# A router's ranks over tiles added up by TensorE in place of VectorE's running sum

## What is computed

```python
xf = input.reshape(N, Dq)
probs = jax.nn.softmax(xf @ router_w + router_b, axis=-1)
eid = jnp.argmax(probs, axis=-1)
onehot = jax.nn.one_hot(eid, E, dtype=xf.dtype)
rank = (jnp.cumsum(onehot, axis=0)[jnp.arange(N), eid] - 1.0).astype(jnp.int32)
valid = rank < C
pos = jnp.where(valid, rank, 0)
vmask = valid.astype(xf.dtype)[:, None]
buf = jnp.zeros((E, C, Dq), xf.dtype).at[eid, pos].add(xf * vmask)
h = jax.nn.relu(jnp.einsum('ecd,edh->ech', buf, w1) + b1[:, None, :])
y = jnp.einsum('ech,ehd->ecd', h, w2) + b2[:, None, :]
y_tok = y[eid, pos] * vmask
yov = jax.nn.relu(xf @ ow1 + ob1) @ ow2 + ob2
out = y_tok + yov * (1.0 - vmask)
```

## Time and profile before

| | us |
|---|---|
| three runs shown | 1013.89, 1017.33, 1018.5 |
| median of them | 1017.33 |
| the profiled execution, its own time | 1013.49 |
| its span in the profile | 1011.7 |

### The profile page before, as it was taken

How to read it: one execution, slowest core, us unless ns; L and a number is a source line. 1 busy time by engine, 2 the same in 40 slices (tenths; PEclk the granted TensorE clock), 3 DMA queues, 4 the chain that set the end, 5 groups by cost and what they waited for, 6 DMA issues and landing times. The chain is left out here.

```text
span 1011.7 us, 17450 instructions
## 1 busy us (share of the span) xinstructions
PE 902.6 (89%) x5825; PEld 642.4 (63%) x5832; DVE 676.6 (67%) x1619; ACT 421.3 (42%) x1133; POOL 376.5 (37%) x279
## 2 busy tenths in 40 slices
PE   2899989999889985868899889999999839999997
PEld 2687744444478864743487547777777517778786
DVE  5899967987689988876377687878768631222221
ACT  2466640000155656753355345556664403122222
POOL 1676402433467722516455313333333410110111
PEclk9999999999999997988899999999999969999999
DMA  6100079999700008102366382311111148534200
GB/s 208 59 1 0 1 205 251 312 306 285 247 1 1 0 1 222 52 16 95 113 188 202 117 262 72 113 51 51 51 51 36 44 143 299 203 98 152 93 12 20
DMA packets 87260, 117.18 MB, mean 116 GB/s; under 512 B 12464, under 2 KB 75949, under 8 KB 86781
## 3 DMA queue, kind: packets, MB, share of 16 engines
q1 hardware_dynamic: 77455, 88.15, 29.4%
q10 hardware_dynamic: 4408, 15.46, 4.6%
q0 software_dynamic: 5328, 12.70, 3.5%
HBM read 68.08 MB, written 50.16 MB: 117 GB/s over the span
## 5 line engine op out<-in xcount | busy, mean ns | idle before, releaser
L1016 PE MATMUL psum<-m_W,lnT 128*128 128x512 f32 x256 | 114.2, 598 | 0.6 <-DVE acc L928 0.6
L410 POOL TENSOR_TENSOR prob<-prob,a_rden 128x1232 f32<-128x1232 f32 x30 | 67.5, 2250 | 58.1 <-DVE a_rden L506 58.1
L1016 PEld LDWEIGHTS psum<-m_W,lnT 128*128 128x128 f32 x256 | 47.2, 190 | 59.0 <-issue 55.8
L2907 ACT ACTIVATE prob<-psum,x_b 128x320 f32<-128x320 f32 x64 | 33.8, 527 | 120.8 <-PE psum L2964 120.8
L2575 PE MATMUL psum<-g_VW,pT 128*128 128x256 f32 (+1 forms) x320 | 72.5, 382 | 1.6 <-ACT pT L2465 1.5
L1001 POOL TENSOR_TENSOR m_masked<-m_rel,m_mrow 128x1232 f32<-128x1232 f32 x16 | 42.2, 2647 | 84.5 <-DMA masked_bias<-m_masked 62.2
L2765 POOL DMA_INDIRECT out_x<-x_yt,x_X x20 | 19.8, 992 | 137.3 <-DVE x_yt L2846 137.3
L2575 PEld LDWEIGHTS psum<-g_VW,pT 128*128 128x128 f32 (+1 forms) x320 | 59.5, 190 | 11.2 <-issue 3.7
L2234 POOL TENSOR_TENSOR g_qr<-g_t 128x1024 f32<-128x1024 f32 x15 | 35.5, 2364 | 74.1 <-DVE g_t L2307 74.1
L2527 PE MATMUL psum<-g_Wq,lnT 128*128 128x512 f32 x128 | 59.1, 605 | 1.0 <-ACT lnT L2439 1.0
L2241 POOL TENSOR_TENSOR prob<-prob,g_rden 128x1232 f32<-128x1232 f32 x15 | 33.7, 2248 | 68.3 <-DVE g_rden L2342 68.3
(11 more groups left out here) (472 smaller groups left out, 2240.7 us busy)
## 6 DMA issues: line engine op xcount, KB each, us to landing
routed_rows<-hole SPq DMA_DIRECT2D x8, 2210.0 KB, 36.8
masked_bias<-m_masked ACTq DMA_DIRECT2D x16, 616.0 KB, 8.2
g_bias<-masked_bias SPq DMA_DIRECT2D x16, 616.0 KB, 3.9
m_xb<-routed_rows SPq DMA_DIRECT2D x39, 130.0 KB, 2.0
m_rel<-in_rel_bias ACTq DMA_DIRECT2D x8, 616.0 KB, 10.9
expert_rows<-hole SPq DMA_DIRECT2D x1, 4680.0 KB, 36.7
g_early_w<-in_L_ffn_w SPq DMA_DIRECT2D x8, 512.0 KB, 4.7
g_early_w<-in_L_ffn_w SPq DMA_DIRECT2D x4, 1024.0 KB, 5.7
```

The lines of the kernel that those rows point to most:

```text
L410: nc.gpsimd.tensor_tensor(heads(c.prob[b]), heads(c.prob[b]), rden[b][:, :].unsqueeze(2).to_broadcast([P, H, SK]), ALU.mult).then_inc(norm ...
L1016: last = nt.matmul(c.ps[p][:, :], c.lnT[b][:, k * P:(k + 1) * P], W[:, k, p * 512:(p + 1) * 512], start=(k == 0), stop=(k == KC - 1))
```

## The change

`first_expert` writes the one-hot rows straight into `r.ohb` as bf16, and its cast is gone. `first_slot` is gone, with the padded buffers and their two memsets. TensorE adds up in one PSUM bank what VectorE's running sum did: for a tile it adds, to the triangular product of the tile itself, the all-ones product of every tile ahead of it. A product with a `shift` covers several tiles at once: columns of the tiles first to last get the counts of the tiles `shift` earlier. `pe_earlier_ranks` issues those that reach into earlier groups (before the group's one-hot rows are ready), `pe_ranks` the triangular one and those inside the group. In the last group one more block of columns, `wide`, gets the total counts.

Products per group: group 0 has 1 + 7 = 8 in place of 2. Group 1 has 11 in `pe_earlier_ranks` (shifts 4 to 8, 1 to 3, 9 to 11) and 1 + 3 = 4 in `pe_ranks`. Group 2 has 16 (shifts 5 to 12, 1 to 4, 13 to 16) and 1 + 4 = 5. `slots` has eight operations: two read PSUM, three are fused scalar-tensor-tensor operations.

```diff
 def first_expert(c, dve, r, u, logits, chain, read, nth=1):
-    lg, tmp, hot = c.lg[:, eights], c.lgt[:, eights], c.gates[:, eights]
+    lg, tmp, hot = c.lg[:, eights], c.lgt[:, eights], r.ohb[:, eights]
...
-    chain(nv.tensor_tensor(tiles(hot), tiles(tmp), wide(first), ALU.is_equal))
-    return nv.tensor_copy(r.ohb[:, eights], hot)
-
-
-def first_slot(c, r, u, chain):
-
-    nv = c.nc.vector
-    n, ones8, _ = group_of(u)
-    pre, first = r.pre, c.first[:, ones8]
-    if u > 0:
-        last_tile = slice((PAD + ROUTED[u - 1][1] - 1) * 8, (PAD + ROUTED[u - 1][1]) * 8)
-        for v in range(2):
-            chain(nv.tensor_copy(pre[v][:, (PAD - 1) * 8:PAD * 8], pre[1][:, last_tile]))
-    chain(nv.tensor_scalar(r.slotf[:, 0:n], first, -float(CAP), float(E3 * CAP), ALU.mult, ALU.add))
+    return nv.tensor_tensor(tiles(hot), tiles(tmp), wide(first), ALU.is_equal)
 
 def slots(c, dve, r, u, ranks, chain, read, nth=1):
...
-    nv.tensor_copy(before, ranks[:, 0:n * 8])
-    nv.tensor_copy(pre[0][:, data], ranks[:, n * 8:2 * n * 8]).then_inc(read, 1)
+    nv.tensor_scalar(over8, ranks[:, 0:n * 8], -float(CAP), 0.0, ALU.add, ALU.max)
+    nv.tensor_tensor(rank8, ranks[:, 0:n * 8], r.ohb[:, eights], ALU.mult).then_inc(read, 1)
     dve.wait_ge(read, nth)
-    chain(nv.tensor_tensor(pre[1][:, data], pre[0][:, data], pre[0][:, back(1)], ALU.add))
-    chain(nv.tensor_tensor(pre[0][:, data], pre[1][:, data], pre[1][:, back(2)], ALU.add))
-    chain(nv.tensor_tensor(pre[1][:, data], pre[0][:, data], pre[0][:, back(4)], ALU.add))
-    chain(nv.tensor_tensor(rank8, before, pre[1][:, back(1)], ALU.add))
-    chain(nv.tensor_scalar(over8, rank8, -float(CAP), 0.0, ALU.add, ALU.max))
-    chain(nv.tensor_tensor(rank8, rank8, hot, ALU.mult))
-    chain(nv.reduce_sum(orank, tiles(over8), AX))
+    nv.reduce_sum(over, tiles(over8), AX)
     chain(nv.reduce_sum(rank, tiles(rank8), AX))
-    chain(nv.tensor_scalar(orank, orank, float(E3 * CAP), None, ALU.add))
-    chain(nv.tensor_scalar(valid, rank, float(CAP), None, ALU.is_lt))
-    chain(nv.tensor_tensor(slotf, slotf, rank, ALU.add))
-    chain(nv.tensor_tensor(slotf, slotf, orank, ALU.subtract))
-    chain(nv.tensor_tensor(slotf, slotf, valid, ALU.mult))
-    return nv.tensor_tensor(r.slot[:, ones8], slotf, orank, ALU.add)
+    chain(nv.scalar_tensor_tensor(out=slotf, in0=c.first[:, ones8], scalar=-float(CAP), in1=rank, op0=ALU.mult, op1=ALU.add))
+    chain(nv.tensor_tensor(slotf, slotf, over, ALU.subtract))
+    chain(nv.scalar_tensor_tensor(out=slotf, in0=rank, scalar=float(CAP), in1=slotf, op0=ALU.is_lt, op1=ALU.mult))
+    return nv.scalar_tensor_tensor(out=r.slot[:, ones8], in0=slotf, scalar=float(E3 * CAP), in1=over, op0=ALU.add, op1=ALU.add)
 
+def rank_tiles(u):
+
+    lo, n = ROUTED[u]
+    return lo, n, n + (lo + n == NT)
+
+def pe_count(c, r, u, bank, shift, first, last, start=False):
+
+    lo = ROUTED[u][0]
+    return c.nc.tensor.matmul(bank[:, (first - lo) * 8:(last - lo) * 8], r.onesb, r.ohb[:, (first - shift) * 8:(last - shift) * 8],
+                              start=start, stop=True, skip_group_check=True)
+
+def pe_earlier_ranks(c, r, u, bank):
+
+    lo, n, wide = rank_tiles(u)
+    shifts = [*range(wide, lo + 1), *range(1, wide), *range(lo + 1, lo + wide)]
+    for shift in shifts:
+        pe_count(c, r, u, bank, shift, max(lo, shift), min(lo + wide, lo + shift), start=shift == shifts[0])
+
 def pe_ranks(c, r, u, bank):
 
-    n, _, cols = group_of(u)
-    c.nc.tensor.matmul(bank[:, 0:n * 8], r.upper, r.ohb[:, cols], start=True, stop=True)
-    return c.nc.tensor.matmul(bank[:, n * 8:2 * n * 8], r.onesb, r.ohb[:, cols], start=True, stop=True)
+    lo, n, wide = rank_tiles(u)
+    c.nc.tensor.matmul(bank[:, 0:n * 8], r.upper, r.ohb[:, lo * 8:(lo + n) * 8], start=u == 0, stop=True, skip_group_check=True)
+    for shift in range(1, wide):
+        last = pe_count(c, r, u, bank, shift, lo + shift, lo + wide)
+    return last
 
...
+                pe.wait_ge(s["s_used"], NT)
+                pe_earlier_ranks(c, r, 1, c.ps[0])
                 pe.wait_ge(s["r_oh_ok"], 2)
-                pe.wait_ge(s["s_used"], NT)
                 pe_ranks(c, r, 1, c.ps[0]).then_inc(s["r_pre_ps"], 1)
...
             first_expert(c, dve, rt, 2, bank_back[:, 0:2 * P], chain, s["lg_read"]).then_inc(s["oh_ok"], 1)
-            first_slot(c, rt, 2, chain)
...
-            chain(nv.tensor_scalar(cnt[:, :], rt.pre[1][0:1, (PAD + NT - LAST - 1) * 8:(PAD + NT - LAST) * 8], -float(CAP), 0.0, ALU.add, ALU.max))
+            chain(nv.tensor_scalar(cnt[:, :], bank_rank[0:1, (NT - LAST) * 8:(NT - LAST + 1) * 8], -float(CAP), 0.0, ALU.add, ALU.max))
...
             pe_logits_back(c, rt, 2, bank_back).then_inc(s["logits_ps"], 1)
+            pe_earlier_ranks(c, rt, 2, bank_rank)
             pe.wait_ge(s["oh_ok"], 1)
             pe_ranks(c, rt, 2, bank_rank).then_inc(s["pre_ps"], 1)
```

More of the change, by code:

```diff
@@ L1118, in __init__ @@
         self.ohb = c.lg2[:, 0:NT * 4].bitcast(BF16)
-        n = (PAD + HALF) * 8
-        self.pre = [c.acc[0][:, u * n:(u + 1) * n] for u in range(2)]
         m = HALF * 8
-        self.before = c.acc[0][:, 2 * n:2 * n + m]
         self.rank8, self.over8 = c.acc[1][:, 0:m], c.acc[1][:, m:2 * m]
-        self.rank, self.valid, self.orank, self.slotf = (c.acc[1][:, 2 * m + u * HALF:2 * m + (u + 1) * HALF] for u in range(4))
+        self.rank, self.over, self.slotf = (c.acc[1][:, 2 * m + u * HALF:2 * m + (u + 1) * HALF] for u in range(3))
         self.slot = c.acc[1][:, 2 * m + 4 * HALF:2 * m + 4 * HALF + NT].bitcast(U32)
@@ L1165, in slots @@
     n, ones8, eights = group_of(u)
[L1166 to L1170, removed]
-    nv.tensor_copy(before, ranks[:, 0:n * 8])
-    nv.tensor_copy(pre[0][:, data], ranks[:, n * 8:2 * n * 8]).then_inc(read, 1)
-    dve.wait_ge(read, nth)
-    chain(nv.tensor_tensor(pre[1][:, data], pre[0][:, data], pre[0][:, back(1)], ALU.add))
-    chain(nv.tensor_tensor(pre[0][:, data], pre[1][:, data], pre[1][:, back(2)], ALU.add))
-    chain(nv.tensor_tensor(pre[1][:, data], pre[0][:, data], pre[0][:, back(4)], ALU.add))
-    chain(nv.tensor_tensor(rank8, before, pre[1][:, back(1)], ALU.add))
-    chain(nv.tensor_scalar(over8, rank8, -float(CAP), 0.0, ALU.add, ALU.max))
-    chain(nv.tensor_tensor(rank8, rank8, hot, ALU.mult))
-    chain(nv.reduce_sum(orank, tiles(over8), AX))
-    chain(nv.reduce_sum(rank, tiles(rank8), AX))
-    chain(nv.tensor_scalar(orank, orank, float(E3 * CAP), None, ALU.add))
-    chain(nv.tensor_scalar(valid, rank, float(CAP), None, ALU.is_lt))
-    chain(nv.tensor_tensor(slotf, slotf, rank, ALU.add))
-    chain(nv.tensor_tensor(slotf, slotf, orank, ALU.subtract))
-    chain(nv.tensor_tensor(slotf, slotf, valid, ALU.mult))
-    return nv.tensor_tensor(r.slot[:, ones8], slotf, orank, ALU.add)
+    rank8, over8 = (t[:, 0:n * 8] for t in (r.rank8, r.over8))
+    rank, over, slotf = (t[:, 0:n] for t in (r.rank, r.over, r.slotf))
+    nv.tensor_scalar(over8, ranks[:, 0:n * 8], -float(CAP), 0.0, ALU.add, ALU.max)
+    nv.tensor_tensor(rank8, ranks[:, 0:n * 8], r.ohb[:, eights], ALU.mult).then_inc(read, 1)
+    dve.wait_ge(read, nth)
+    nv.reduce_sum(over, tiles(over8), AX)
+    chain(nv.reduce_sum(rank, tiles(rank8), AX))
+    chain(nv.scalar_tensor_tensor(out=slotf, in0=c.first[:, ones8], scalar=-float(CAP), in1=rank, op0=ALU.mult, op1=ALU.add))
+    chain(nv.tensor_tensor(slotf, slotf, over, ALU.subtract))
+    chain(nv.scalar_tensor_tensor(out=slotf, in0=rank, scalar=float(CAP), in1=slotf, op0=ALU.is_lt, op1=ALU.mult))
+    return nv.scalar_tensor_tensor(out=r.slot[:, ones8], in0=slotf, scalar=float(E3 * CAP), in1=over, op0=ALU.add, op1=ALU.add)
 def pe_logits(c, r, u, bank):
@@ L2363, in route @@
                 row_statistics(c, 0)
-                for u in range(2):
-                    nv.memset(r.pre[u][:, 0:PAD * 8], 0.0)
                 dve.wait_ge(s["r_in"], 16 * 3)
@@ L2379, in places @@
                 first_expert(c, dve, r, 0, c.ps[1][:, 0:2 * P], chain, s["r_lg_read"]).then_inc(s["r_oh_ok"], 1)
-                first_slot(c, r, 0, chain)
             if t == RANKS_AT:
@@ L2384, in places @@
             if t == HALF + 7:
-                first_slot(c, r, 1, chain)
                 dve.wait_ge(s["r_pre_ps"], 2)
```

## The result

Over 20 executions each, the median went from 1016.31 us to 1012.49 us. The ratio of the changed kernel to the one before is 0.9969, with a 95% interval from 0.9954 to 0.9984. On 1016.3 us that is 3.2 us less, between 1.6 and 4.7; the two medians differ by 3.8. One execution of the changed kernel, 1370.38 us at a mean granted clock of 0.652, is left out of the ratio. The forecast was 2.7 us less and 1014.6 us, with a range from 1010.5 to 1018: a small gain, and one under 0.5%. Both came true.

A forecast was written before the change was run, and what follows sets the result against it. The last router's serial VectorE chain ahead of the experts' matmuls was taken to bound the kernel, with TensorE limiting attention. Router 2.15 plus attention 0.52 made 2.7 us, so 1017.33 became 1014.6 us, range 1010.5 to 1018.

The forecast's parts named there:

- a longer wait for the landing: Last router: prediction wrong if the wait for the scatters' landing grows by what VectorE's chain lost.
- Part 1: Last router up to the ranks: removing the cast and `first_slot` starts `slots` 0.32 us earlier.
- Part 2: Last group's `slots`: 1.46 us in place of 3.29, a gain of 1.83 us.
- Part 3: First group inside attention: VectorE 2.2 us earlier, but TensorE's warming products let only 1.04 us through.
- Part 4: Second group inside attention: 13 more TensorE products on the path cost 0.52 us at 0.04 each.
- The clock: First expert's matmuls: moving their start could give back up to 1.7 us of half-clock loss or cost as much again.
- M: Rival: small TensorE products cost 0.07 us each; gain 2.0 us, 1015.3 us; chance 0.17.
- B: Rival: small TensorE products cost 0.11 us each; net gain 0.7 us, 1016.6 us; chance 0.14.
- D: Rival: load and product do not overlap, 0.29 us per small product; loss 6.3 us, 1023.6 us; chance 0.04.
- C: Rival: the clock over the first expert gives its stall back; gain 4.4 us, 1012.9 us; chance 0.14.
- its opposite: Rival: the clock over the first expert loses 1.7 us more, 1016.3 us; chance 0.07.
- E: Rival: last router gains nothing as said because GpSimd was not waiting for VectorE's chain; chance 0.02.

The follow-up runs named there:

- warm2: The changed kernel with 2 warming products in place of 10 ahead of the last attention tile's scores; ratio 0.9953 to the kernel before.
- the first pair: First traces of the kernel before and the changed kernel; the first expert's 32 matmuls took 10.32 and 11.75 us.
- the second: Both kernels traced again without edit; the first expert's 32 matmuls took 11.24 us before and 8.85 us changed.

## Why the prediction was right, and where it was off

**What bounds.** Right. The last router is a series in which VectorE's operations arrive one to one. The scatter came 0.27 us behind the chain before and after. Nothing took the place of what was removed: the first expert's matmuls came 13.91 us behind that scatter before and 13.37 after, so the sign against the forecast, a longer wait for the landing, did not show.

**Part 1, start of the chain.** Forecast 0.32 us, measured 2.42 - 2.06 = 0.36 (turned-back logits to `slots`, 811.77 to 814.19 and 811.15 to 813.21). The step is right. The price of 0.04 us per small product was too high: the last of the five started 0.10 us behind the first (812.89, then four over 812.93 to 813.17), not 0.16. The sixteen earlier products cost nothing, as said.

**Part 2, `slots`.** Forecast 1.46 us, measured 1.39. The gain was 1.90, not 1.83. The fused operations take 0.16 us, no more than the two-tensor ones of that width, and reading PSUM cost nothing.

**Part 3, first group.** The mechanism held: VectorE's chain was shorter, the rotation now starts at 774.30 when TensorE's queries end (770.58 + 3.68), and the warming products cap the gain, which warm2 showed. The rotation starts 2.85 us earlier (16.74 and 13.89 behind the start of A), where I had 2.2; behind the warming products that changed nothing. The stall I foresaw is there too: L1157 took 0.88 us, until GpSimd's multiply ended, as L1174 took 1.32 in the earlier trace rows. The Trainium skill ("GPSIMD Engine Reference", section "1. Specifications") says that VectorE contends with GpSimd for SBUF where it has two SBUF inputs, and the trace agrees: the sums just ahead, with one input, were not held up. The size was off: the scores start 1.49 us earlier, not 1.04. Two terms were missing. The first is 0.27 us ahead of the queries. I had booked that idle time as cover for six products and called the removed cast and `first_slot` of the first group "hidden by TensorE". They were not: their 0.42 us on VectorE bring ScalarE's copy L2439 forward by as much (from 10.02 to 9.60 us behind the start of A), and it was this copy that TensorE waited for. The products took back the other 0.15. The second is 0.18 us: the idle time shown ahead of the scores was 1.04, but more was to be had. Scores without a wait start at 785.61, which is 0.16 ahead of the last warming product's modelled end, 785.77; with the wait they started 1.05 behind it (784.62 and 785.67).

**Part 4, second group.** On the path, as forecast, but its cost was mis-sized. With 0.52 us I had 13 times 0.04. Before:

```profile
795.41 0.18 PE L1219 MATMUL psum<-lg,choice 128*128 128x32 bf16 x1
...
797.61 4.48 PE L2575 MATMUL psum<-g_VW,pT 128*128 128x256 f32 x20
```

After:

```profile
795.25 0.42 PE L1198 MATMUL psum<-lg,choice 128*128 128x32 bf16 x11
...
797.68 4.49 PE L2567 MATMUL psum<-g_VW,pT 128*128 128x256 f32 x20
```

Counted from the scores of tile 15, the last tile's products with the values start 797.61 - 785.67 = 11.94 us later before and 797.68 - 785.61 = 12.07 after: 0.13 us. The thirteen products themselves cost 0.28: from the first rank product to the last tile's transposes it was 795.93 - 795.41 = 0.52 us and is 796.05 - 795.25 = 0.80. The other 0.15 came back around them: 0.10 between the scores and the ranks (the scores behind the wait took 2.36 us, without it 2.26), and 0.05 in the transposes, which had waited for VectorE's L2346.

**The sum.** 2.15 + 0.52 = 2.7 was forecast; 2.26 + 1.36 = 3.6 is what the rows give, 3.2 (1.6 to 4.7) what the times give. Nearly all of the miss is attention, 0.84 us: 0.27 + 0.18 in part 3, and 0.39 in part 4. Two mistakes make up most of it, a price taken at the cautious side of a pair of rows (0.24 us in part 4), and an idle time booked as cover without asking whether its releaser moves too (0.27). The rest, 0.33, lies around the waits that are gone: TensorE's work behind each of them started or ran later than its idle time tells. All of them made the forecast too small, and none hid another. Of the 2.1 us between the forecast's 1014.6 and the median of 1012.49, 1.0 is the level it started from, 1017.33 as the median of three executions, where twenty have 1016.31.

**The clock.** It was put in the range and not in the sum, and that was right: in the first pair it cost the changed kernel 1.4 us, in the second it gave 2.4. It can be bought back with warming products, which I had not looked for.

**The rivals.** M and B (0.07 and 0.11 us per product) and D (0.29) are excluded by the 0.02 to 0.03 of every stream. C and its opposite are both seen, one in each pair, as chance and not as outcomes of the change. E fell with the first chain.

## What to carry to other kernels

Where an idle time of one engine is to serve as cover for added work, follow its releaser first: if the change moves that releaser as well, the idle time is gain to be had and not cover. A stream of small bf16 products with 32 to 64 columns costs TensorE 0.025 us each here, so sums over tiles that VectorE does in chained steps of 0.2 us are cheap there, most of all where TensorE idles. When executions scatter by more than the change, measure stretches between two rows of a trace: here A and B repeated to 0.01 us while the start of A moved by 13. Not every stretch does so: C, under a changing clock, moved by 2.9 with no edit.

## What was not expected of the hardware

Small products with a load of weights each stand 0.025 us apart over streams of 16 and 40 at full clock (16 in 0.56 us, 40 in 1.15 us, the last one's duration of 0.18 included). Nine warming products after TensorE's idle were not enough to keep the clock through the first expert: part of C ran at half clock in seven of eight traces, in five of them after the clock had already been full, and C was 10.3 to 11.8 us there, 8.85 where the clock was full. From TensorE's first logit product to ScalarE's copy it was 1.10 or 1.81 us with no edit near it. Executions of one kernel differ by some 10 us, and the granted clock goes with it: 0.962 and less at 1020 us, 0.967 and more at 1013.
